# Scores of two heads side by side on TensorE's rows, and the two maxima tiles of a step apart

## The reference, cut to what matters

```python
b, t, d = x.shape                       # 2, 1024, 128;  H = 16 heads of HD = 8
q, k, v = (proj(Wq, bq), proj(Wk, bk), proj(Wv, bv))
q = q * cos + rotate_half(q) * sin
k = k * cos + rotate_half(k) * sin
scale = 1.0 / jnp.sqrt(jnp.asarray(HD, x.dtype))
attn = jnp.einsum('bhqd,bhkd->bhqk', q, k) * scale
attn = jax.nn.softmax(attn, axis=-1)
out = jnp.einsum('bhqk,bhkd->bhqd', attn, v)
```

## Time and profile before

| | |
|---|---|
| median of 3 runs | 906.85 us |
| profiled execution | 907.05 us, its span 905.3 us |
| TensorE busy | 779.2 us, 86% |
| VectorE busy | 794.6 us, 88% |
| ScalarE busy | 686.4 us, 76% |
| GpSimd busy | 239.9 us, 27% |
| mean granted clock of TensorE | 0.94 |

### The profile page before, as it was taken

The page is one execution under the profiler, slowest core; times in us unless marked ns, Lnnn a source line. Parts: engine busy times, 40 slices in busy tenths (PEclk is TensorE's granted clock), DMA queues, the critical chain, the costliest instruction groups (busy, mean ns, idle before and its releaser), DMA issues.

```text
span 905.3 us, 12616 instructions
## 1 busy us (share of the span) xinstructions
PE 779.2 (86%) x4297; PEld 414.1 (46%) x4312; DVE 794.6 (88%) x752; ACT 686.4 (76%) x1298; POOL 239.9 (27%) x136
## 2 busy tenths in 40 slices
PE   7789999999999999999666677677575899999998
PEld 3312222212122122225445556666575688888886
DVE  5998899998899899997997979999999887888765
ACT  2406888888788788886557799999998578888884
POOL 3800000000000000010001357898986701422000
PEclk9958999999999999999798788999998899999999
DMA  5313132312122220011001334565554202222101
GB/s 136 89 46 100 50 107 69 106 53 74 36 81 67 65 60 13 13 40 47 0 1 25 118 122 149 181 218 187 186 174 149 89 24 71 94 71 70 56 37 47
DMA packets 41467, 75.16 MB, mean 83 GB/s; under 512 B 7588, under 2 KB 25324, under 8 KB 40764
## 3 DMA queue, kind: packets, MB, share of 16 engines
q1 hardware_dynamic: 41404, 74.36, 26.0%
HBM read 64.71 MB, written 8.31 MB: 81 GB/s over the span
## 4 chain that ended last, share of the span: by engine, by line
PE 50%; DVE 27%; ACT 11%; issue 9%; POOL 2%; DMA 0%; DVEq 0%; ACTq 0%; POOLq 0%
PE ps L1680 9%; PE ps L1707 9%; DVE nmax_k L1240 7%; PE ps L1969 6%; PE ps L1970 6%; PE ps L1971 6%; ACT dtb L1075 5%; PE ps L1651 4%; DVE hst L1409 4%; DVE nmax L1237 3%; ACT abar L1049 2%; PE ps L1867 2%; PE ps L1913 2%; PE ps L1790 1%; ACT prob L937 1%
## 5 line engine op out<-in xcount | busy, mean ns | idle before, releaser
L937 ACT ACTIVATE prob<-ps 128x512 f32<-128x512 f32 x512 | 272.5, 599 | 90.4 <-PE ps L1680 88.4
L1240 DVE TENSOR_REDUCE nmax_k<-ps 128x2 f32<-128x1024 f32 x224 | 262.3, 1219 | 28.2 <-PE ps L1651 27.0
L1680 PE MATMUL ps<-qs,ks 96*128 96x512 bf16 x512 | 159.4, 387 | 3.9 <-ACT prob L937 2.6
L862 POOL TENSOR_TENSOR hc<-hst,cbr 128x1024 f32<-128x1024 f32 x63 | 151.2, 2422 | 43.3 <-DVE hst L1409 22.7
L1409 DVE TENSOR_TENSOR_SCAN hst<-abar,ps 128x1024 f32<-128x1024 f32 x64 | 142.8, 2272 | 4.4 <-issue 1.9
L1707 PE MATMUL ps<-prob,vq 128*16 128x512 f32 x1024 | 134.6, 597 | 0.1
L1523 DVE TENSOR_TENSOR act_l<-act_t,act_h 128x1024 fp32r<-128x1024 f32 x64 | 91.8, 1444 | 34.5 <-ACT act_h L1172 34.5
L1075 ACT ACTIVATE dtb<-dtxt,bt 128x128 f32<-128x128 f32 x352 | 107.4, 394 | 2.9 <-PE ps L1867 2.9
L1680 PEld LDWEIGHTS ps<-qs,ks 96*128 96x128 bf16 x512 | 34.0, 97 | 153.0 <-ACT prob L937 121.7
L1168 ACT ACTIVATE act_t<-ps,b1t 128x512 f32<-128x512 f32 x128 | 81.8, 681 | 25.3 <-PE ps L1971 25.2
L1867 PE MATMUL ps<-ident,dtb 128*128 128x128 f32 x352 | 54.6, 303 | 45.7 <-DVE hst L1409 37.2
(11 more groups left out here) (221 smaller groups left out, 1125.1 us busy)
## 6 DMA issues: line engine op xcount, KB each, us to landing
cbr<-s_dram SPq DMA_DIRECT2D x64, 512.0 KB, 3.9
gate<-c_dram SPq DMA_DIRECT2D x5, 1024.0 KB, 4.7
qs<-q_dram SPq DMA_DIRECT2D x16, 288.0 KB
ks<-k_dram SPq DMA_DIRECT2D x48, 96.0 KB
o_dram<-o_sb SPq DMA_DIRECT2D x14, 256.0 KB, 2.4
gate<-c_dram SPq DMA_DIRECT2D x6, 512.0 KB, 4.0
wf<-in_L_ffn_w SPq DMA_DIRECT2D x8, 256.0 KB, 5.0
wfq<-in_L_ffn_w SPq DMA_DIRECT2D x8, 256.0 KB, 4.9
```

The source lines that it names most:

```text
L862: nc.gpsimd.tensor_tensor(hc[:, m % RING], hst[:, m % RING], cbr[:, m % RING], ALU.mult).then_inc(s_hc, 1)
L937: nc.scalar.activation(prob[:, n % 8], ps[:, 4 + (first + n) % 3], ACT.Exp, scale=ATT_SCALE).then_inc(s_exp, 1)
L1240: nc.vector.tensor_reduce(nmax_k[:, half, kk, 2 * pair:2 * pair + 2, qt], ps[:, 2 * pair:2 * pair + 2, :], AX.X, ALU.max, negate=True).the ...
L1680: nc.tensor.matmul(ps[:, 4 + (first + n) % 3], ks[p][:, kt // 4, j, kt % 4 * P:(kt % 4 + 1) * P], qs[p][:, half, j, :], start=True, stop=T ...
```

## The change

Three things change together.

- The stacks. `PAIRED` keeps six of the nine products of parts, so a head has 48 rows of products and two of maxima (`ROWS` = 50). Heads 0 and 2 lie in rows 0 to 49, heads 1 and 3 in rows 64 to 113 (`side`). The parts are stored in DRAM once for each of their six places (`first_copies`, `copy_to`), and `fill` goes: GpSimd sets the whole `ks` to one.
- The order. One tile of maxima stands behind score products 0 and 1, the other behind 2 and 3; the value products stay last.
- The queues. SP loads heads with two DMAs a half instead of twelve. The maxima rows of the upper side are stored by GpSimd (`s_prow`), those of the lower by SP; TensorE waits for both. GpSimd also stores the parts of the second batch entry.

```diff
+PAIRED = ((0, 2), (0, 0), (0, 1), (1, 0), (1, 1), (2, 0))
+PROD = len(PAIRED) * HD
+ROWS = PROD + 2
+SIDE = 64
...
+        def side(h, rows=ROWS):
+            return slice(SIDE * (h % 2), SIDE * (h % 2) + rows)
+        def maxima_rows(p, half, n, z):
+            return qs[p][SIDE * n + PROD:SIDE * n + ROWS, half].rearrange("r h (q t) -> r (h q) t", t=P)[:, :, 32 * z:32 * z + 32]
...
+            def store_rest(u):
+                sp.wait_ge(s_part3, u + 1)
+                for copy in range(len(PAIRED)):
+                    sp.dma_start(*copy_to(u, copy, slice(1, QUAD))).then_inc(s_parts_out[u], 16)
             def load_heads(it, p, f):
+                for t, to in ((k_dram, km), (q_dram, qm)):
+                    sp.dma_start(to[p][:, f], t[it, f, 1:5].rearrange("n (d h) t -> h (n d) t", h=QUAD)).then_inc(s_qm[p], 16)
+            def load_stack(stack, dram, it, f, done):
+                for n in range(2):
+                    sp.dma_start(stack[side(n, PROD), f], dram[it, f].rearrange(
+                        "n (d h m) t -> m (n d) h t", d=HD, m=2)[n]).then_inc(done, 16)
...
+            for u, part in ((0, 0), (1, 0), (0, 1), (2, 0), (0, 2), (1, 1), (1, 2)):
+                store_first(u, part)
+            sp.wait_ge(s_parts_out[0], STORES)
+            load_stack(qs[0], q_dram, 0, 0, s_first)
...
-            nc.gpsimd.memset(fill[:, 0], 0.0)
-            nc.gpsimd.memset(fill[:, 1], 1.0).then_inc(s_fill, 1)
+            nc.gpsimd.memset(ks[0][:], 1.0).then_inc(s_set[0], 1)
...
+            def store_maxima(it, p, half):          # on GpSimd
+                pool.wait_ge(s_nmax, 2 * it + half + 1)
+                for z in range(4):
+                    pool.dma_start(maxima_rows(p, half, 1, z), nmax_t[32 * z + 16:32 * z + 32, half, :]).then_inc(s_prow[half], 16)
...
             for p in range(SETS):
                 values(p, p)
+            for n in range(1, SETS):
+                nc.gpsimd.memset(ks[n][:], 1.0).then_inc(s_set[n], 1)
+            store_second_batch(range(CHUNKS, 2 * CHUNKS))
+            store_maxima(0, 0, 0)
+            for it in range(PASSES):
+                store_maxima(it, it % SETS, 1)
+                if it + 1 < PASSES:
+                    store_maxima(it + 1, (it + 1) % SETS, 0)
+                if it + SETS < PASSES:
+                    pool.wait_ge(s_pv, STEPS * (it + 1))
+                    values(it + SETS, it % SETS)
...
                     if kt == 0:
                         pe.wait_ge(s_nrow[half], 64 * (it + 1))
+                        pe.wait_ge(s_prow[half], 64 * (it + 1))
...
-                        nc.tensor.matmul(ps[:, 4 + (first + n) % 3], ks[p][:, kt // 4, j, kt % 4 * P:(kt % 4 + 1) * P],
-                                         qs[p][:, half, j, :], start=True, stop=True).then_inc(s_st, 1)
-                        for tile in todo if j == 1 else ():
+                        nc.tensor.matmul(ps[:, 4 + (first + n) % 3], ks[p][side(j), kt // 4, j // 2, kt % 4 * P:(kt % 4 + 1) * P],
+                                         qs[p][side(j), half, j // 2, :], start=True, stop=True).then_inc(s_st, 1)
+                        for tile in todo[j // 2:j // 2 + 1] if j % 2 else ():
```

More of the change, by code:

```diff
@@ L38 @@
 PARTS = 3
-PROD = PARTS * PARTS * HD
-ROWS = 96
+PAIRED = ((0, 2), (0, 0), (0, 1), (1, 0), (1, 1), (2, 0))
+COPIES = tuple(tuple(slice(r[0], r[-1] + 1, r[1] - r[0] if len(r) > 1 else 1) for r in
+                     ([n for n, pair in enumerate(PAIRED) if pair[kind] == part] for part in range(PARTS))) for kind in range(2))
+PROD = len(PAIRED) * HD
+ROWS = PROD + 2
+SIDE = 64
 ATT_SCALE = 1.0 / float(np.sqrt(np.float32(HD)))
@@ L133, in build_kernel @@
         parts = sb("parts", [P, 6, PARTS, BANK], BF16)
-        fill = sb("fill", [4 * (ROWS - PROD), 2, 2 * BANK], BF16)
-        blank = fill[:, 0, 0:BANK]
-        stacks = [[sb(f"{w}{n}", [ROWS, 2, QUAD, BANK], BF16) for w in ("qs", "ks")] for n in reversed(range(SETS))][::-1]
+        stacks = [[sb(f"{w}{n}", [P, 2, QUAD // 2, BANK], BF16) for w in ("qs", "ks")] for n in reversed(range(SETS))][::-1]
         qs, ks = ([pair[n] for pair in stacks] for n in range(2))
@@ L259, in build_kernel @@
         s_nrow = [sem(f"s_nrow{n}") for n in range(2)]
+        s_prow = [sem(f"s_prow{n}") for n in range(2)]
         s_st = sem("s_st")
@@ L366, in part, with first_copies, copy_to @@
             return parts[:, u, n] if u < 6 else num_b[:, (PARTS * (u - 6) + n) * BANK:(PARTS * (u - 6) + n + 1) * BANK]
+        def side(h, rows=ROWS):
+            return slice(SIDE * (h % 2), SIDE * (h % 2) + rows)
+        def maxima_rows(p, half, n, z):
+            return qs[p][SIDE * n + PROD:SIDE * n + ROWS, half].rearrange("r h (q t) -> r (h q) t", t=P)[:, :, 32 * z:32 * z + 32]
+        def first_copies(u, part):
+            c, kind = PIECES[u]
+            dst = (q_dram, k_dram)[kind][0, c % 2, COPIES[kind][part]]
+            src = part_rows(u, slice(0, QC))[:, part].unsqueeze(1)
+            return dst.rearrange("n c t -> c n t"), src.to_broadcast([QC, dst.shape[0], BANK])
+        def copy_to(u, copy, groups):
+            c, kind = PIECES[u]
+            dst = (q_dram, k_dram)[kind][4 * (c // 2) + groups.start:4 * (c // 2) + groups.stop, c % 2, copy]
+            return dst, part_rows(u, slice(QC * groups.start, QC * groups.stop))[:, PAIRED[copy][kind]]
         def part_rows(u, rows):
@@ L607, in load_heads @@
             def load_heads(it, p, f):
[L609 to L615, removed]
@@ L842, in _ @@
                 values(p, p)
-            with pool.Fori(1, PASSES // SETS) as r:
-                for p in range(SETS):
-                    pool.wait_ge(s_pv, STEPS * (SETS * (r - 1) + p + 1))
-                    values(SETS * r + p, p)
-            for p in range(PASSES % SETS):
-                pool.wait_ge(s_pv, STEPS * (SETS * (PASSES // SETS - 1) + p + 1))
-                values(PASSES - PASSES % SETS + p, p)
+            for n in range(1, SETS):
[9 more added lines that the diff above has]
+                    values(it + SETS, it % SETS)
             norm_pool(1, 0)
@@ L1639, in score_half @@
                     pe.wait_ge(s_max, 32 * it + t - 1)
-                mm = nc.tensor.matmul(ps[:, 2 * (t % 2) + kk], qs[p][:, half, h, q * P:(q + 1) * P],
-                                      ks[p][:, kk, h, :], start=True, stop=True)
+                mm = nc.tensor.matmul(ps[:, 2 * (t % 2) + kk], qs[p][side(h, PROD), half, h // 2, q * P:(q + 1) * P],
+                                      ks[p][side(h, PROD), kk, h // 2, :], start=True, stop=True)
                 if kk == 1:
```

109 lines of the change are left out of this document (46 added, 63 removed).

## The result

The changed kernel takes 960.45 us (median of four runs: 949.96, 953.43, 967.47, 1098.02) against 906.09 for the kernel before on the same chip; the ratio over the two short runs is 1.050 (95% interval 1.045 to 1.055). The forecast was 923, with a range of 897 to 944: right in sign, far too small. The long runs are told of here because part of the cause lies in them: their mean granted clock is 0.735 and 0.894, that of the short ones 0.912 and 0.928. The profiled execution took 953.43, its span is 951.6, 46.3 more than before.

The account below looks back on a forecast made before the run. It took a chain of waits, almost all on TensorE and closed by the wait for one of three PSUM banks, to bound the kernel. 907.05 + 12.0 (GpSimd's queue) + 4.4 (steps) = 923.45, so 923 us, range 897 to 944.

Parts of the forecast that it names:

- The ring: In each attention step product 3 waits for product 0's exponential (three PSUM banks): 2.71 us a step, +4.4 us in all.
- the ring doesn't bind: Rival: product 3 finds its bank free, VectorE bounds the step at 2.49 us; 895 us, or 883; chance 0.14.
- Side by side: Score products of two heads in separate rows run together: 0.33 us a pair, 0.21 less, twice a step.
- what side by side saves turns into a wait: Within a step, the time saved on paired score products becomes a wait of 0.42 us before product 3.
- POOL's queue: At the start GpSimd issues 24 stores before its first maxima, landed at 81.2 where TensorE started at 69.24: +12.0 us.
- 2.0 to land: Time for GpSimd's last maxima store of the first half to arrive after its issue: 2.0 us.
- The issue price: Cost of each DMA issue by GpSimd, taken as 1.0 us, between 0.43 and 2.0; named as likeliest to fail.
- SP's queue: SP's changed loads and extra stores at the start and in later passes: nothing added to the time.
- the first heads are wanted at 85: Store transfers at the start take 30 us, to about 69, before the first heads are wanted at 85: nothing added.
- The later halves: After the first half, GpSimd's maxima land at 10.1 us into a half, needed at 10.84: hidden by 0.7.
- the first steps: First pass's steps with whole tiles of maxima: 2.81 us each, nothing added, at most 0.2 each either way.

Follow-up runs that it names:

- e2_order: Kernel before with only the new order, one tile of maxima behind products 0 and 1, the other behind 2 and 3: 913.01 us, ratio 1.0043.
- e15_spread_pad: e10_spread with the products behind the exponentials over 64 rows instead of 50: 891.08 us, ratio 0.9813.
- e3_side_only: Changed kernel with both tiles of maxima behind product 1 again and SP's stores split by group and part as in e1_split: 914.68 us, ratio 1.0077.
- e10_spread: e6_best with GpSimd's 24 second-batch stores issued six at a time behind four halves' maxima: 896.56 us, ratio 0.9886.
- e8_pool_late: Changed kernel with GpSimd's 24 stores moved behind the maxima of pass 0's second half: 979.85 us.
- e6_best: e1_split with old order, only group 1 stored before heads and maxima, GpSimd's 24 stores behind the maxima of pass 0's second half: 902.2 us.
- e1_split: Changed kernel with SP's stores of groups 1 to 3 as 36 DMAs, one per group and part, in place of 24: 1007.98 us.
- e7_one_side: e6_best with all heads in rows 0 to 49, so products can't run side by side: 1102.87 us.
- e11_padded: e7_one_side with the products behind the exponentials over 96 rows instead of 50, the added rows zeros against ones: 924.4 us.
- e14_spread_apart: e10_spread with the change's new order, the two tiles of maxima apart: 930.25 us (910.99 to 1000.47).
- e16_apart_pad: e14_spread_apart with the products behind the exponentials over 64 rows instead of 50: 913.26 us.
- e13_pad64: Changed kernel with the products behind the exponentials over 64 rows instead of 50: 951.73 us.
- e12_spread_warm: e10_spread with 16 products without use, over 128 rows, between the first score tiles and pass 0: 896.2 us.
- e4_three: Kernel before with its stores of groups 1 to 3 of the first batch entry as 12 DMAs, three groups outermost: 911.88 us, ratio 1.0036.

## Why the prediction failed, step by step

**The ring: right**, in mechanism and size: 2.70 for 2.71, +4.6 for +4.4, shown alone by e2_order. Its rival, that the ring doesn't bind, is out: with the exponentials and banks as they are, 0.34 of a step is a wait for `prob` at product 3, and in no kernel did the 111 steps take the 2.49 each of that rival (2.56 at the least, in e15_spread_pad).

**Side by side: right**, 0.32 for 0.33. That "what side by side saves turns into a wait" was right too, and e3_side_only and e10_spread show what was left lying: in the old order most steps are 2.37 to 2.44, and the 111 take 285.

**POOL's queue: nearly the right delay, by two errors that cancel.** 1.0 an issue was taken, 0.70 measured (0.56 for maxima), so its maxima are out at 69.2, not 79.2. The term "2.0 to land" was wrong the other way: the last of them took 16.7, with the 24 stores ahead of it in its own queue, and landed at 85.4 where the forecast had 81.2. With the stores moved behind them, the maxima landed in 4.5 at most (e8_pool_late) and 1.9 (e6_best). So this queue alone would have held TensorE to 85.4, some +16 for the +12.0. That is worked out, not run, and it is luck that the two are near. The issue price, named as the likeliest to fail, did; the landing, which was not named, failed by more.

**SP's queue: the step that failed.** It said "nothing", on two grounds. One was a size: 30 us of transfer, ended at 69, at the 182 GB/s of a busy stretch. From 43 to 69 the rate was 114 GB/s with DMA engines busy by 0.53; the stores were issued until 89.95 and landed 6.5 later. The other was a fault of reasoning, and the worse one: it held "the first heads are wanted at 85" as the time to beat. But the loads of heads stand in SP's queue ahead of the maxima of the first half, and those were due at 64.22. With the forecast's own figures: stores landed at 69, heads 2.3, maxima 2.7, landing 2.0, so 76, which is 7 late where 0 was written down. I had asked when the data of the wait are used, not who stands behind it. The runs bear it out: TensorE starts at 105.55 with all of it, at 83.6 with GpSimd's stores out of the way (e8_pool_late), at 90.05 with SP's stores in another form (e1_split), and at 67.2 with only group 1 ahead, the other form and GpSimd's stores behind (e6_best). So of the 36.3, some 16 would have come from GpSimd's maxima as well, and SP's queue, put down as nothing, adds the 20 from 85.4 to 105.5.

**The later halves: right**; from 107 to 430 us no wait of TensorE on a transfer is in the trace, and the maxima of GpSimd land 1.7 (median) behind their issue there.

**Not in the forecast: the clock.** It costs 4 us in the profiled run, where the first steps had been put at nothing, and up to 145 in others. That 50 rows can leave TensorE at 1.2 GHz is shown by e7_one_side against e11_padded and, with heads side by side, by e14_spread_apart against e16_apart_pad on one chip (three long runs of five against none of five); e13_pad64 says the same of the changed kernel (none of five against two of four). The kernel before, with 96 rows, shows 1.00. With heads side by side it took the new order as well: in the old order with 50 rows none of 24 runs fell (e3_side_only, e6_best, e10_spread, e12_spread_warm; clocks 0.912 to 0.938), and in the new order none of the 6 with 96 rows did (e2_order).

Not settled: why the fall comes in some runs and not in others of one kernel, and why the old order, side by side, escapes it with 50 rows. Why SP's store takes 2.1, and GpSimd's maxima up to 16.7 to land, while GpSimd's stores are under way is argued from shared DMA engines and a queue in order; the runs show only that both go away with these stores.

## What to carry to other kernels

For a wait put in a queue, the time to beat is that of the most urgent thing behind it, not that of the data it waits for; and a small transfer behind large ones in its queue can land when they have, not in its own time, as GpSimd's maxima did. Before packing products into fewer rows to save time, look at the granted clock of the packed version in several runs; filling the rows up with zeros is free in columns and took away the scatter here, worth 5 to 17 us in the median and nothing to 5 between short runs. A packing that shortens one engine's share pays only in an order that keeps work inside the shadow of the wait that closes the step: the same layout gave most steps at 2.40 or at 2.70.

## What the runs showed of the hardware

- Products of 50 rows, one behind the other, at 1.2 GHz for all of attention (granted 0.50, TensorE busy 180.00 of 180.00), with a mean clock of 0.72 over the kernel in all five runs (e7_one_side); over 96 rows 0.95 in the same stretch and 0.93 over the kernel in four runs, though the rows more were zeros (e11_padded).
- A store of 96 KB from SP took 0.43 of its queue alone (kernel before), 1.06 with three groups outermost (e4_three), 1.26 in the changed kernel's form without GpSimd's stores (e8_pool_late) and 2.1 with them; an issue from GpSimd 0.70 for 128 KB and 0.56 for 1 KB. GpSimd's stores landed 6.3, 8.5, 10.8 and 12.5 us behind their issue, by piece, and the four 1 KB transfers behind them 10.4 to 16.7; with nothing ahead of them these took 1.7 to 1.9 (e6_best).
